# One of four low-part subtractions of a layer-one attention unit goes from GpSimd to VectorE

## The reference

```python
scores = jnp.einsum('bqhd,bkhd->bhqk', q, k) * scale
attn = jax.nn.softmax(scores, axis=-1)
out = jnp.einsum('bhqk,bkhd->bqhd', attn, v)
```

```python
buf = jnp.zeros((E, capacity, D), dtype=xf.dtype).at[routes, pos].set(xf)
y = jnp.einsum('ecd,efd->ecf', buf, expert_w) + expert_b[:, None, :]
out = jnp.where(keep[:, None], gathered, xf) * route_probs[:, None]
```

## Time and profile before

| what | value |
| --- | --- |
| median of 3 runs | 7328.2 us (7327.3 to 7329.21) |
| the profiled execution's own time | 7343.86 us |
| its span, first to last instruction | 7342.1 us |
| mean granted TensorE clock, share of full speed | 0.912 |
| PE busy | 6310.8 us (86%) |
| DVE busy | 4485.6 us (61%) |
| ACT busy | 3195.6 us (44%) |
| POOL busy | 2512.4 us (34%) |

### The profile page before, as it was taken

The page is one execution under the profiler, slowest core; times in us unless marked ns, Lnnn a source line. Parts: engine busy times, 40 slices in busy tenths (PEclk is TensorE's granted clock), DMA queues, the critical chain, the costliest instruction groups (busy, mean ns, idle before and its releaser), DMA issues.

```text
span 7342.1 us, 124751 instructions
## 1 busy us (share of the span) xinstructions
PE 6310.8 (86%) x39399; PEld 4073.3 (55%) x39399; DVE 4485.6 (61%) x11034; ACT 3195.6 (44%) x6291; POOL 2512.4 (34%) x2135
## 2 busy tenths in 40 slices
PE   6798897988979889798997979889898897988986
PEld 4556565655646556564664646556465564655643
DVE  4465665656656566565656656566565665656664
ACT  2354453544435345353443534444344443544531
POOL 3434242333323333233332323323233332333300
PEclk8899898998989999898998989989899897989987
DMA  2131221202112111121212212122120211211100
GB/s 63 32 72 24 56 44 43 48 20 65 34 48 44 46 36 36 46 52 41 44 26 56 44 38 44 26 56 44 40 45 23 67 34 48 44 34 48 36 27 8
DMA packets 91264, 308.93 MB, mean 42 GB/s; under 512 B 27030, under 2 KB 32102, under 8 KB 80358
## 3 DMA queue, kind: packets, MB, share of 16 engines
q1 hardware_dynamic: 90598, 300.55, 17.9%
HBM read 49.33 MB, written 41.94 MB: 12 GB/s over the span
## 4 chain that ended last, share of the span: by engine, by line
issue 53%; POOL 28%; PE 13%; DVE 3%; DMA 1%; POOLq 1%; ACT 0%; SPq 0%; DVEq 0%; ACTq 0%
POOL pr_lo L456 22%; POOL on L1178 2%; PE bank L753 2%; PE bank L780 2%; PE bank L739 2%; PE bank L795 1%; PE bank L778 1%; PE bank L796 1%; PE bank L809 1%; DVE hm L1458 1%; DMA stacks<-parts 1%; POOL h L1156 1%; DVE mxh L1468 1%; POOL rs L1153 1%; PE bank L647 1%
## 5 line engine op out<-in xcount | busy, mean ns | idle before, releaser
L1468 DVE TENSOR_REDUCE mxh<-bank 128x1 f32<-128x512 f32 x4096 | 2778.1, 688 | 1765.8 <-PE bank L753 1739.3
L1032 ACT ACTIVATE pr<-bank 128x512 f32<-128x512 f32 x4096 | 2405.4, 596 | 2324.4 <-PE bank L780 2289.4
L456 POOL TENSOR_TENSOR pr_lo<-pr 128x1024 bf16<-128x1024 f32 x992 | 1877.2, 1893 | 1491.5 <-ACT pr L1032 1491.5
L753 PE MATMUL bank<-stacks 128*128 128x512 f32 x4096 | 1770.3, 437 | 207.6 <-DVE mxh L1468 172.8
L780 PE MATMUL bank<-stacks 65*128 65x512 f32 (+1 forms) x4096 | 1893.8, 464 | 9.3 <-ACT pr L1032 9.2
L795 PE MATMUL bank<-v,pr 128*128 128x129 bf16 x8192 | 1088.7, 226 | 106.9 <-POOL pr_lo L456 94.3
L778 PE MATMUL bank<-stacks 128*128 128x512 f32 x2048 | 1118.0, 546 | 45.2 <-issue 40.4
L753 PEld LDWEIGHTS bank<-stacks 128*128 128x128 f32 x4096 | 831.7, 204 | 582.3 <-DVE mxh L1468 354.4
L796 PE MATMUL bank<-v,pr_lo 128*128 128x129 bf16 x7936 | 1038.3, 224 | 0.0
L795 PEld LDWEIGHTS bank<-v,pr 128*128 128x128 bf16 x8192 | 799.0, 100 | 403.9 <-issue 350.1
L780 PEld LDWEIGHTS bank<-stacks 65*128 65x128 f32 (+1 forms) x4096 | 814.0, 199 | 295.9 <-issue 176.3
(11 more groups left out here) (178 smaller groups left out, 5049.0 us busy)
## 6 DMA issues: line engine op xcount, KB each, us to landing
stacks<-parts SPq DMA_DIRECT2D x384, 512.0 KB, 6.7
parts_d<-pr SPq DMA_DIRECT2D x16, 2048.0 KB, 6.9
stacks<-parts_d SPq DMA_DIRECT2D x224, 128.0 KB, 3.0
stacks<-parts_d SPq DMA_DIRECT2D x224, 64.0 KB, 2.7
stacks<-mrow SPq DMA_DIRECT2D x512, 2.0 KB
out<-hm SPq DMA_DIRECT2D x16, 512.0 KB, 2.7
stacks<-pr SPq DMA_DIRECT2D x32, 128.0 KB, 5.9
stacks<-pr SPq DMA_DIRECT2D x32, 64.0 KB, 3.7
```

The lines of the kernel that those rows point to most:

```text
L456: return eng.tensor_tensor(low_of(seg.kind, u, kt - 1).rearrange("p a b -> p (a b)"), w, hi, ALU.subtract)
L753: mm(maxb[k % 2][:, :], qs[:, t * P:(t + 1) * P], ks[:, g * HALF:(g + 1) * HALF], start=True, stop=True).then_inc(max_filled.sem, 1)
L1032: act.activation(pr[:, at % 2, kt, :], score[k % 2][:, :], ACT.Exp, scale=SCALES[layer]).then_inc(exp_done.sem, 1)
L1468: dve.tensor_reduce(mxh[:, layer, n // 2, n % 2:n % 2 + 1], maxb[k % 2][:, :], AX_X, ALU.max)\
```

## The change

The fourth pair of every layer-one unit is subtracted by DVE instead of POOL, with the same `lo_parts`. On DVE it stands at step 0 of the next unit, ahead of that step's max reduces. It has a semaphore of its own, `lo_last`, and PE's first value product waits for both counts.

```diff
-        lo_done = Counts(sem("lo_done"), 16 * 4)
+        lo_done = Counts(sem("lo_done"), 16 * 3)
+        lo_last = Counts(sem("lo_last"), 16)
...
                 if j == 0:
-                    te.wait_ge(lo_done.sem, lo_done.at(seg.l0, 4 * (u + 1)))
+                    te.wait_ge(lo_done.sem, lo_done.at(seg.l0, 3 * (u + 1)))
+                    te.wait_ge(lo_last.sem, lo_last.at(seg.l0, u + 1))
...
                     if layer == 0 and kt in LO_STEPS:
                         lo_parts(pool, seg, at, kt - 1).then_inc(lo_done.sem, 1)
-                    elif kt == 0 and at > 0 and units_of(seg.kind)[at - 1][0] == 0:
-                        lo_parts(pool, seg, at - 1, T - 1).then_inc(lo_done.sem, 1)
...
-                if seg.kind == "first":
-                    lo_parts(pool, seg, at, T - 1).then_inc(lo_done.sem, 1)
...
             def attention(seg, *beside):
                 for step, at, layer, u, kt in steps_of(seg.kind):
+                    if kt == 0 and at > 0 and units_of(seg.kind)[at - 1][0] == 0:
+                        lo_parts(dve, seg, at - 1, T - 1).then_inc(lo_last.sem, 1)
                     for tile in due_tiles(seg.kind, step):
                         max_tile(seg, "now", *tile)
...
                 at = len(units_of(seg.kind)) - 1
+                if seg.kind == "first":
+                    lo_parts(dve, seg, at, T - 1).then_inc(lo_last.sem, 1)
                 for jj in range(2):
                     outputs(seg, at, jj)
```

## The result

The changed kernel takes 7380.9 us (median of four runs, 7376.6 to 7387.84), the kernel before 7327.75 us beside it (7319.12 to 7329.21). The ratio is 1.0076, with a 95% interval of 1.0058 to 1.0093: slower by some 53 us. The profiled execution of the changed kernel took 7380.36 us with a span of 7378.6 us, 36.5 us more than the span of before (7342.1 us), at a mean granted clock of 0.910 instead of 0.912.

A forecast was written before the change was run, and what follows sets the result against it. PE, 86% busy, waits for POOL's pairs (94.3 us) and DVE's expert operations (202.3 us). Terms +55 -16 -22 -9 = +8, clock +18, total +26 on 7328.2: 7354 us, range 7316 to 7400.

The forecast's parts named there:

- The likeliest case: Slower, from kind B plus more falls of the clock: 7354 us, chance 0.45.
- kind B: Units with experts ahead and none behind, five per pass in 14 passes: value product 0.79 us later, +55 us.
- the clock: One in four of 70 kind B units falls to 1.2 GHz, +28 us; shorter stops save 10; +18.
- The price of the pair: The pair on DVE takes 1.22 us and pushes what follows by 1.14 us; lower bound 0.81 us.
- The rival of a short pair: The pair takes only 0.81 us on DVE, so the kernel gets faster: 7271 us, chance 0.13.
- Kind A: Units with no experts near: the wait for POOL becomes a wait for the reduce, 81 places, -16 us.
- Kind C: Units with experts ahead and behind: expert products on PE cover the pair with 0.8 us to spare, costing nothing.
- Kind D: Start of a loop turn: one `norm_apply` stand behind POOL's third pair falls away, 1.6 us each, -22 us.
- Kind E: Last layer-one unit of a pass, no max tiles behind: PE starts 0.63 us earlier, 15 places, -9 us.
- The second wait: PE's second semaphore wait costs at most 0.08 us at 150 places, up to +12 us; taken as 0.
- The transfer to the median: The profiled execution before lay 15.7 us above the median of runs; the difference was taken to carry over.
- The port: At kind A the pair may stand behind POOL's scaling L1186: +30 us, 7384 us; chance 0.05.

The follow-up runs named there:

- The spare reduce: Kernel before, all pairs on POOL, plus an unread DVE maximum over 1024 elements of expert weights at the 70 kind B places: 7460.7 us, ratio 1.0172.
- The experiment at kind D alone: Against the kernel before, DVE takes the fourth pair only at place 0 of each loop turn and "penult" (14 places): 7313.63 us, ratio 0.9973.
- the eleven kernels above: The kernel before, the change, and nine variants in pair placement, order, spare reduce or start shift, one trace each: medians from 7257.01 to 7460.7 us.

## Why the prediction was right, and where its sizes were off

The likeliest case came out: slower, by kind B and by the clock, with 7380.9 us inside the range and 27 us above the forecast of 7354. That the number lies inside is partly luck: the clock's term was too small and stood at the wrong units, and with two spare memsets ahead the same change measures 7404 us, above the range's 7400. The kernel without the pair at kind B confirms the main term, the loss there.

**The price of the pair** was estimated at 1.22 us from a slope between other operations; it is 1.216. The rival of a short pair (0.81 us) falls with it.

**Kind B**, predicted +55 us (0.79 each), measured +53.8. At full clock the value product comes 4.29 us after the first score product instead of 3.49, 0.80 each. The spare reduce shows that the mechanism is DVE's time ahead of the reduces.

**Kind A**, predicted -16, measured -14.4. The second-pass units give 0.15 each where the prediction worked out 0.16. At full clock the loop's give 0.22 to 0.23.

**Kind C's pair** was costed at nothing, and is hidden: units at full clock stand at 4.98 us before and after. The +45.4 us there are the clock's.

**Kind D**, predicted -22, measured -29.7. The mechanism is right, but the term was read from one turn, and the prediction looked for 3.6 us of `norm_apply` where 11 of the 14 turns have 2.13. Read instruction by instruction, `norm_apply` had two operations held up behind POOL's pairs in six of the 14 turns and one in the other eight, 20 in all; after the change there are three in all. Seventeen of these fell away, not fourteen, because POOL's remaining two pairs often end before DVE gets there. A part of the 29.7 is the clock's: with no operation held up the value product comes 5.6 us after the first score product at full clock (six turns) and 6.5 to 6.7 where the clock is low (five turns). Six turns at about 1 us are some 6 us, an estimate from these.

**Kind E**, predicted -9, measured -10.4.

**The second wait** was bounded at 12 us and taken as nothing. The experiment at kind D alone puts it at 0.05 us a place in the second pass, and at 5.5 us over the kind A units.

**The clock** was the term that was mis-sized and misplaced. The prediction had 17 more falls at kind B, less 10 us for shorter stops elsewhere, +18 in all. Measured is one fall fewer at B and 28 more at C. All that isn't a shift at kinds A, B, D or E (-0.7 us together) is 36.9 + 0.7 = +37.6 us of the span: +45.6 at C, +10.5 behind the units of kind A (in the stretches of place 4 low clock starts 13 times, before once) and +2.0 at B, less 16.4 behind E, mostly between the passes, and 4.1 at D. C's part goes with kind B: 41 falls become 12 when only kind B's pair goes back to POOL. Kind A's part doesn't: in that kernel low clock still starts 12 times at place 4, and in all six kernels with kind A's pair on DVE 6 to 13 times, in the five with it on POOL once to five times. The prediction had no term for it. Here the Trainium skill ("TensorE: Matmul & The Clock Gate", section "Part 1: The HAM clock gate"), by which recent activity sets the clock, agrees in kind at kinds B and C: ahead of each of the 50 falls of the changed kernel PE has stood for about 1.4 us or more in the 5 us before. In the 5 us ahead of the 13 at place 4 it has no stop above 0.15 us, and no run here shows what sets them off.

**The transfer to the median** cost the other part of the miss. The prediction let the 15.7 us by which the profiled execution of before lay above its median carry over. The profiled execution of the changed kernel lies on its median (7380.36 against 7380.9), so spans differ by 36.5 us and medians by 53.

**The port**, a rival at 7384 us, happens to name nearly the measured time, but not by its mechanism: at kind A the pair comes 0.16 us ahead of the scaling L1188, and the scaling stands, 1.21 us instead of 0.29. Nobody waits for it: the shift at A is what was worked out without any loss to the port.

What stays open is why it is kind C that falls in the changed kernel and B as well when it starts 2 us later. The stops at C are the same 1.44 us in kernels with 12 falls and with 41. That DVE's work at B brings more falls at B and C is shown by the eleven kernels above, in one trace each; how the stops of successive units add up to a fall is not.

## What to carry to other kernels

An operation that moves to an idler engine is paid where it stands in that engine's queue, so its place matters more than its speed: here 1.2 us on DVE cost 0.8 us at the seventy places where DVE was already the late engine, and won elsewhere. Split such a move by the kinds of place in the schedule and leave out the one that loses; that turned +0.8% into -0.5%, and one reduce ahead of the moved operation into -1.0%, with some help of the clock. In this kernel, whose TensorE stops for 1.44 us at each unit with experts ahead, the clock added about as much again as the loss that was worked out directly (38 us to 54; with the pair at kind B alone 49 to 58, the second wait and kind D's 7 us included; with the spare reduce 63 to 58), and much of it at other units than those that were changed. In a kernel of that kind it needs a term of its own.

## What the runs showed of the hardware that was not expected

Two memsets ahead of the first pass went with 23 us more on the changed kernel and with nothing that can be told on the kernel before. So a few tens of microseconds between two variants of such a kernel may come from where its stops fall in time; that this is the reason here is argued, not shown.

Of two forms of DVE operation that met a running pair of POOL, one was held up and the other wasn't. `norm_apply` (TENSOR_SCALAR, float32 from and to SBUF) took 1.8 to 2.0 us instead of 0.33; the spare reduce over 1024 elements of SBUF took its 1.21 us in the midst of a POOL pair, whose 992 instances took 1889 to 1932 ns in that kernel. And POOL is held up behind DVE too: L1188 takes 547 ns in the mean of the changed kernel and its counterpart L1186 293 ns before, here as they stand among the groups of the trace of before and of after.

```profile
L1186 POOL TENSOR_TENSOR on<-on,o_r 128x64 f32<-128x64 f32 x256 | 74.9, 293 | 543.4 <-DVE on L1504 543.2
```

```profile
L1188 POOL TENSOR_TENSOR on<-on,o_r 128x64 f32<-128x64 f32 x256 | 140.0, 547 | 540.5 <-DVE on L1502 540.2
```

That agrees with what the Trainium skill ("SBUF — State Buffer", section "SBUF: two separate sides") states of the port that the two engines share: whichever starts first keeps it for the whole instruction.
